# The last stage of a two-layer graph network: y0 in a second one-hot, edge weights two pairs ahead, both tiles in one VectorE instruction

## The reference, cut to what matters

```python
x0, x1 = _lin_irreps(x0, x1, W_up0, W_up1)        # 128 scalars and 128 x 3 vectors per node
tpw = h @ W_mlp4 / jnp.sqrt(...)                  # h: (E, 64), a radial network of edge_attr_8
w1, w2, w3, w4 = jnp.split(tpw, 4, axis=-1)       # 128 each
s0, s1 = x0[sender], x1[sender]
y0, y1 = edge_attrs[:, 0:1], edge_attrs[:, 1:4]
p1 = w1 * s0 * y0
p2 = (w2 * s0)[:, :, None] * y1[:, None, :]
p3 = w3[:, :, None] * s1 * y0[:, None, :]
p4 = w4 * jnp.einsum('eum,em->eu', s1, y1) / SQRT3
msg0 = segment_sum(concat([p1, p4]), receiver)
msg1 = segment_sum(concat([p2, p3]), receiver)
o0, o1 = _lin_irreps(msg0, msg1, W_out0, W_out1)
```

## Time and profile before

| what | value |
|---|---|
| median of 3 runs | 5701.41 us (5696.20 to 5704.77) |
| the profiled execution | 5664.33 us, span of the core 5662.4 us |
| granted TensorE clock, mean of the span | 0.938 |
| PE busy | 4809.4 us (85%) |
| VectorE (DVE) busy | 2867.7 us (51%) |
| ScalarE (ACT) busy | 2291.3 us (40%) |
| GpSimd (POOL) busy | 2726.7 us (48%) |
| chain that ended last | PE 30%, issue 24%, DVE 11%, DVEq 8%, ACT 7%, ACTq 7% |

### The profile page before, as it was taken

How to read it: one execution, slowest core, us unless ns; L and a number is a source line. 1 busy time by engine, 2 the same in 40 slices (tenths; PEclk the granted TensorE clock), 3 DMA queues, 4 the chain that set the end, 5 groups by cost and what they waited for, 6 DMA issues and landing times.

```text
span 5662.4 us, 106923 instructions
## 1 busy us (share of the span) xinstructions
PE 4809.4 (85%) x17040; PEld 2243.0 (40%) x17041; DVE 2867.7 (51%) x8231; ACT 2291.3 (40%) x6164; POOL 2726.7 (48%) x3492
## 2 busy tenths in 40 slices
PE   7898566778898878887788899999999999998998
PEld 5443122333343223333344444444444444444444
DVE  7543122334453111123344577777777777777676
ACT  0442000111112223431223466666666666666565
POOL 0333666776664655456666344433333333333332
PEclk9998677899998889998899999999999999999999
DMA  2233666777776767667777444444433343333333
GB/s 83 95 106 112 178 191 205 222 227 234 238 246 191 214 207 220 195 208 236 249 254 267 148 119 115 116 116 118 120 112 115 117 120 113 115 117 113 113 117 95
DMA packets 433675, 916.83 MB, mean 162 GB/s; under 512 B 63093, under 2 KB 170869, under 8 KB 433510
## 3 DMA queue, kind: packets, MB, share of 16 engines
q0 software_dynamic: 195840, 641.89, 38.0%
q1 hardware_dynamic: 182918, 245.65, 13.0%
q10 hardware_dynamic: 54880, 28.91, 1.7%
HBM read 787.79 MB, written 128.41 MB: 162 GB/s over the span
## 4 chain that ended last, share of the span: by engine, by line
PE 30%; issue 24%; DVE 11%; DVEq 8%; ACT 7%; ACTq 7%; POOL 4%; DMA 3%; another core or an unknown queue 3%; POOLq 2%; SPq 0%
PE bank L1267 8%; POOL ring L544 4%; PE bank L1392 3%; PE bank L1223 3%; PE bank L1225 3%; ACT hB L788 3%; ACTq L785 3%; ACT dense_w L799 3%; DVEq L1110 2%; DVE hA L1118 2%; DVE hA L1104 2%; DVEq L1120 2%; DMA ef<-in_ef_t_dram 2%; PE bank L1310 2%
## 5 line engine op out<-in xcount | busy, mean ns | idle before, releaser
L544 POOL DMA_INDIRECT ring<-tab_d,idx x1568 | 1549.7, 988 | 817.4 <-issue 523.2
L1392 PE MATMUL bank<-dense_w,oh 128*128 128x512 f32 x3520 | 1618.6, 602 | 71.2 <-DVE dense_w L1127 70.3
L1267 PE MATMUL bank<-ring,ohp 128*128 x3904 | 1105.4, 436 | 462.0 <-POOLq L556 226.2
L510 POOL DMA_INDIRECT ring<-up_d,idx x880 | 856.7, 973 | 498.5 <-POOL idx L506 348.4
L799 ACT ACTIVATE dense_w<-hA,hC 128x128 f32<-128x128 f32 x2640 | 820.0, 389 | 664.4 <-DVE hA L1118 599.5
L1392 PEld LDWEIGHTS bank<-dense_w,oh 128*128 128x128 f32 x3520 | 632.8, 189 | 863.0 <-issue 666.7
L1267 PEld LDWEIGHTS bank<-ring,ohp 128*128 x3904 | 411.3, 107 | 1134.2 <-issue 866.0
L1015 DVE TENSOR_TENSOR ohp<-iota_w,dst_f 128x512 f32 x392 | 266.5, 692 | 679.8 <-PE bank L1267 246.3
L506 POOL COPY idx<-src_i 128x2 int32 x440 | 80.5, 183 | 1054.3 <-DVE dense_w L1127 1012.2
L1382 PE MATMUL bank<-w,hC 64*128 64x256 f32 x3520 | 504.6, 404 | 31.5 <-issue 20.9
L1104 DVE SCALAR_TENSOR_TENSOR hA<-ring,hC,hB 128x128 f32<-128x128 f32 x880 | 270.9, 349 | 500.9 <-ACT hB L788 436.6
(11 more groups left out here) (180 smaller groups left out, 4917.6 us busy)
## 6 DMA issues: line engine op xcount, KB each, us to landing
hC<-hid_d SPq DMA_DIRECT2D x440, 64.0 KB
tab_d<-tout SPq DMA_DIRECT2D x98, 256.0 KB, 2.8
tw<-tab_d SPq DMA_DIRECT2D x98, 256.0 KB
hlw<-hl_d SPq DMA_DIRECT2D x98, 256.0 KB
ring<-tab_d,idx POOLq DMA_INDIRECT x1568
hid_d<-hC ACTq DMA_DIRECT2D x98, 256.0 KB
hl_d<-agg SPq DMA_DIRECT2D x74, 256.0 KB, 3.1
ring<-up_d,idx POOLq DMA_INDIRECT x880
```

Of the source, the lines that this page charges most:

```text
L510: g_.indirect_dma_start(ring_v[:, b, k, :], None, table, bass.IndirectOffsetOnAxis(idx_t[:, b, k:k + 1], 0)).then_inc(S["got"][b], 16)
L544: g_.indirect_dma_start(ring_h[:, b, k, :], None, table, bass.IndirectOffsetOnAxis(idx_b[:, b, k:k + 1], 0)).then_inc(S["got"][b], 16)
L1267: ins = pe.matmul(bank[0][:, :], ohp_b[:, bass.ds(at, 1), k, :].rearrange("p b n -> p (b n)"), ring_b[:, bass.ds(slot, 1), k, h, :].rearra ...
L1392: ins = pe.matmul(bank[h][:, :], oh[:, b, k, :], msg[:, b, k, h, :], start=False, stop=False, skip_group_check=True)
```

## The change

PSUM becomes one tensor `ps` of eight banks, so that an instruction may take both tiles' banks at once. The edge weights of a pair go into two neighbouring banks, and there are two such sets (banks 2 and 3, 4 and 5); PE issues them 512 columns wide, behind the sum of the pair two back. ScalarE no longer makes `w13`; it makes `oh0` = one-hot * y0 (two, 128 wide), and PE sums the half with p1 and p3 with `oh0` and the half with p4 and p2 with `oh`. VectorE starts a pair with the one-hot, `t2` and p1, goes on with q1, a drain and q2, then p3 for each tile, a drain and p4; it takes both tiles in one instruction for `t2`, p1 and p4; p3 reads w3 from PSUM. The zero matmuls that closed a window's banks go, the last sum closes them itself. In the order of windows, the second pair of each window is written out ahead of `copy_mT(w-1)`, and PE has the first two steps written out ahead of `out_product`. The minimum number of pairs in a window is now 4 (`MINV`).

The diff, cut to its core; its parts are in the order PSUM, ScalarE (`weigh`, `window`), VectorE (`messages`), PE:

```diff
+MINV = 4
-        bank = [ctx.enter_context(nc.psum_tensor(f"bank{i}", [P, D], F32)) for i in range(8)]
+        ps = ctx.enter_context(nc.psum_tensor("bank", [P, 8, D], F32))
+        bank = [ps[:, i, :] for i in range(8)]
-        w_bank = [[bank[2], bank[3]], [bank[7], bank[5]]]
-        m_bank = [bank[4], bank[6]]
+        w_bank = [ps[:, 2:4, :], ps[:, 4:6, :]]
+        m_bank = [bank[6], bank[7]]
...
-                    ac.wait_ge(M["w_done"], n + 2)
-                    ac.wait_ge(M["u_used"], n + (NU - 1))
-                    for k in range(2):
-                        ins = ac.mul(w13[:, k, :], w_bank[k][0][:, 0:2 * P], yg[:, b, 4 * k:4 * k + 1])
-                    ins.then_inc(M["w13"], 1)
                     ac.wait_ge(M["t2"], n)
                     ac.wait_ge(M["seg_done"], n)
                     for k in range(2):
                         for m in range(3):
-                            ins = ac.mul(msg[:, b, k, 1, P + m * P:2 * P + m * P], t2[:, k, :],
-                                         yg[:, b, 4 * k + 1 + m:4 * k + 2 + m])
+                            ac.mul(msg[:, b, k, 1, P + m * P:2 * P + m * P], t2[:, b, k, :],
+                                   yg[:, b, 4 * k + 1 + m:4 * k + 2 + m])
+                    for k in range(2):
+                        ins = ac.mul(oh0[:, b, k, :], oh[:, b, k, :], yg[:, b, 4 * k:4 * k + 1])
                     ins.then_inc(M["p2"], 1)
...
+                second_pair(w)
+                if not isinstance(w, int) or w > 0:
+                    copy_mT(w - 1)
                 rest(w)
                 if not isinstance(w, int) or w < NW - 1:
                     first_pair(w + 1)
                 keep_a(w)
-                copy_mT(w)
...
+                    w = w_bank[b]
+                    ve.wait_ge(M["seg_done"], n)
+                    ve.tensor_tensor(oh[:, b, :, :], iota_w[:, :].unsqueeze(1).broadcast_to([P, 2, P]),
+                                     dst_f[:, bass.ds(g * 2, 2)].unsqueeze(2).broadcast_to([P, 2, P]), ALU.is_equal)
+                    ve.wait_ge(M["got"][ub], ve.snap((n + (NU - 1)) // NU * 32))
+                    ve.wait_ge(M["w_done"], n + 2)
+                    ve.tensor_tensor(t2[:, b, :, :], w[:, :, 2 * P:3 * P], u[:, :, 0:P], ALU.mult).then_inc(M["t2"], 1)
+                    ve.tensor_tensor(msg[:, b, :, 0, 0:P], w[:, :, 0:P], u[:, :, 0:P], ALU.mult)
                     ve.wait_ge(M["q0"], n)
...
-                    ve.wait_ge(M["p2"], n)
                     for k in range(2):
-                        ins = ve.tensor_tensor(t2[:, k, :], w_bank[k][1][:, 0:P], u[:, k, 0:P], ALU.mult)
-                    ins.then_inc(M["t2"], 1)
-                    ve.drain()
-                    for k in range(2):
-                        ins = ve.tensor_tensor(msg[:, b, k, 1, 0:P], q2[:, k, :], w_bank[k][1][:, P:2 * P], ALU.mult)
-                    ins.then_inc(M["w_read"], 1)
-                    ve.wait_ge(M["w13"], n + 1)
-                    for k in range(2):
-                        ve.tensor_tensor(msg[:, b, k, 0, 0:P], w13[:, k, 0:P], u[:, k, 0:P], ALU.mult)
+                        ve.tensor_tensor(msg[:, b, k, 0, P:].rearrange("p (m u) -> p m u", m=3),
+                                         w[:, k, P:2 * P].unsqueeze(1).broadcast_to([P, 3, P]),
+                                         u[:, k, P:4 * P].rearrange("p (m u) -> p m u", m=3), ALU.mult)
                     ve.drain()
+                    ve.tensor_tensor(msg[:, b, :, 1, 0:P], q2[:, :, :], w[:, :, 3 * P:4 * P], ALU.mult).then_inc(M["u_used"], 1)
...
-                pe.wait_ge(M["w_read"], n)
-                pe.wait_ge(M["w13"], n)
-                for h in range(2):
-                    for k in range(2):
-                        ins = pe.matmul(w_bank[k][h][:, 0:2 * P], hid[k * HID:(k + 1) * HID, b, :],
-                                        w4[k * HID:(k + 1) * HID, h * 2 * P:(h + 1) * 2 * P], start=True, stop=True)
+                if not isinstance(n, int):
+                    pe.wait_ge(M["u_used"], n + (NU - 2))
+                for k in range(2):
+                    ins = pe.matmul(w_bank[b][:, k, :], hid[k * HID:(k + 1) * HID, b, :],
+                                    w4[k * HID:(k + 1) * HID, :], start=True, stop=True)
...
+                        ins = pe.matmul(bank[h][:, :], (oh0, oh)[h][:, b, k, :], msg[:, b, k, h, :], start=False,
+                                        stop=(last and k == 1), skip_group_check=True)
...
+                def one(b):
+                    sum_pair(n, b, last)
+                    if ahead:
+                        edge_weights(n + 2, b)
...
+                step(True)
+                if not isinstance(w, int) or w < NW - 1:
+                    step(True)
+                    if not isinstance(w, int) or w > 0:
+                        out_product(w - 1)
+                    with pe.Fori(lo + 2, hi - 1) as g:
+                        step(True)
+                    step(True, True)
-                touch(bank[0][:, :], D, False)
-                touch(bank[1][:, :], D, False).then_inc(M["sum_done"], 1)
```

More of the change, by code:

```diff
@@ L176, in build @@
         yg = hC[:, 1, 0:16].rearrange("p (b n) -> p b n", b=2)
-        w13 = hA[:, 0, :].rearrange("p (k n) -> p k n", k=2)
-        t2, q1 = (hA[:, 1, i * 256:(i + 1) * 256].rearrange("p (k n) -> p k n", k=2) for i in range(2))
+        t2 = hA[:, 0, :].rearrange("p (b k n) -> p b k n", b=2, k=2)
+        q1 = hA[:, 1, 0:256].rearrange("p (k n) -> p k n", k=2)
+        oh0 = yb[:, :].rearrange("p (b k n) -> p b k n", b=2, k=2)
         q2 = hB[:, 0, 0:256].rearrange("p (k n) -> p k n", k=2)
@@ L809, in first_pair, with second_pair @@
                 weigh(lo)
+            def second_pair(w):
+                weigh(ac.snap(lo_r) + 1)
             def rest(w):
-                with ac.Fori(ac.snap(lo_r) + 1, ac.snap(hi_r)) as g:
+                with ac.Fori(ac.snap(lo_r) + 2, ac.snap(hi_r)) as g:
                     weigh(g)
             def keep_a(w):
-                ac.wait_ge(M["sum_done"], w + 1)
+                more = 1 if isinstance(w, int) and w == NW - 1 else 0
+                ac.wait_ge(M["seg_done"], ac.snap(c) + more)
                 after(ac, M["turned"], w)
@@ L822, in copy_mT @@
                 after(ac, M["o_done"], w)
-                ac.copy(mT[:, 0:4, :], bank[4][:, :].rearrange("p (c n) -> p c n", c=4)).then_inc(M["mT_a"], 1)
+                ac.copy(mT[:, 0:4, :], m_bank[0][:, :].rearrange("p (c n) -> p c n", c=4)).then_inc(M["mT_a"], 1)
             def window(w):
+                second_pair(w)
+                if not isinstance(w, int) or w > 0:
+                    copy_mT(w - 1)
                 rest(w)
@@ L1138, in first_pair, with second_pair @@
                 messages(lo)
+            def second_pair(w):
+                messages(ve.snap(lo_r) + 1)
             def rest(w):
-                with ve.Fori(ve.snap(lo_r) + 1, ve.snap(hi_r)) as g:
+                with ve.Fori(ve.snap(lo_r) + 2, ve.snap(hi_r)) as g:
                     messages(g)
@@ L1147, in keep_b @@
             def keep_b(w):
-                ve.wait_ge(M["sum_done"], w + 1)
+                more = 1 if isinstance(w, int) and w == NW - 1 else 0
+                ve.wait_ge(M["seg_done"], ve.snap(c) + more)
                 after(ve, M["turned"], w)
@@ L1178, in _ @@
             over_windows(ve, window)
+            copy_mT(NW - 1)
             finish(NW - 1)
@@ L1391, in sum_pair @@
                     for h in range(2):
-                        ins = pe.matmul(bank[h][:, :], oh[:, b, k, :], msg[:, b, k, h, :], start=False, stop=False,
-                                        skip_group_check=True)
+                        ins = pe.matmul(bank[h][:, :], (oh0, oh)[h][:, b, k, :], msg[:, b, k, h, :], start=False,
+                                        stop=(last and k == 1), skip_group_check=True)
                 ins.then_inc(M["seg_done"], 1)
@@ L1417, in out_product, with step @@
                 ins.then_inc(M["o_done"], 1)
-            def weights_ahead():
+            def step(ahead, last=False):
                 n = pe.snap(c)
-                def step(b):
-                    edge_weights(n, b)
-                    sum_pair(n - 1, 1 - b)
-                pick(pe, pe.snap(n % 2), 0, 2, step)
+                def one(b):
+                    sum_pair(n, b, last)
+                    if ahead:
+                        edge_weights(n + 2, b)
+                pick(pe, pe.snap(n % 2), 0, 2, one)
                 pe.reg_add(c, c, 1)
```

42 lines of the change are left out of this document (16 added, 26 removed).

## The result

| | median, us | runs | against the kernel before (95%) |
|---|---|---|---|
| before, beside it | 5703.1 | 5696.2 to 5709.4 | |
| after | 5534.7 | 5512.9 to 5543.1 | 0.9699 [0.9669, 0.9729] |

The profiled execution after took 5543.1 us (span 5541.2).

The account below looks back on a forecast made before the run. A chain between VectorE and ScalarE was taken as the bound, with PE nearly full. Plain pairs -22 us, window changes -82, 5 given back: 5602 us against the median 5701.4; 8-in-10 range 5500 to 5715.

Parts of the forecast that it names:

- The ring: Last stage: VectorE waits for ScalarE's q0 (411 us), ScalarE's products for VectorE's t2 (584 us); the change cuts this.
- PE's own repeat of 4.60: PE in a plain pair: edge weights to sum 1.07 us plus the sum 3.53 us, so PE alone could repeat in 4.60.
- The restart of 1.5: VectorE, from issuing p4 to the next pair's first instruction: taken as 1.5 us, bounds 1.14 and 1.9, mostly open time.
- my own range: Forecast's range for the whole time, with the restart between 1.3 and 1.65 us and window bounds: 5540 to 5670 us.
- VectorE becomes the bound and the plain repeat hardly moves: Plain pairs of the last stage: VectorE's 4.90 us over PE's 4.60, against 4.95 before, giving -22 us.
- The first rival: Plain pairs: PE is the bound because the restart hides; repeat 4.60 us, 5477 us in all, chance 0.13.
- Edge weights to sum 1.07, side by side: PE, four 512-column edge-weight instructions with the two 64-row halves running together: 1.07 us, bounds 0.95 to 1.8.
- Changes of window 4.1 us: Last stage: each change costs 4.1 us extra instead of 5.8, 48 x -1.7 = -82 us, bounds -43 and -120.
- The 5 us given back: Added to the summed -104 us for the one-hot's wait and addresses: 5 us.
- Code fetch, 0.10: Rival: VectorE's window code is fetched again, 1.3 to 2.8 us per window, +61 to +132 us, 5663 to 5734; chance 0.10.
- The dearer restart: Rival: VectorE takes 1.9 us from p4 to the next pair, repeat 5.27 us, 5760 us; chance 0.09.
- the halves lose their overlap: Rival: PE's 64-row edge-weight halves no longer run side by side at 512 columns, repeat 5.25 us, 5793 us; chance 0.03.

Follow-up runs that it names:

- t2 first, alone: The kernel before with only t2 moved to the head of the pair, in two buffers: 5572.5 us, ratio 0.9807.
- the run with one wide product less: The changed kernel with the wide product p3 made for the first tile alone, so part of the messages is left out: 5483.6 us, ratio 0.9612.
- tile by tile: The changed kernel with t2, the first product and p4 made in two 128-column instructions each instead of one of 256: 5621.5 us, ratio 0.9875.
- second one-hot: The changed kernel with VectorE writing one more one-hot of the same kind to scratch in each pair: 5920.2 us, ratio 1.0378.

## Why the prediction was right or wrong

- *The ring is cut.* Right: t2 first, alone, gave the plain repeat its whole gain.
- *PE's own repeat of 4.60.* Short by 0.09. I read the sum's 3.53 up to a zero matmul; up to the 64-row edge weights it is 3.63. The earlier trace rows already showed 3.60 (4008.39 to 4011.99), and the prediction does not use it.
- *The restart of 1.5.* This term failed. It is 1.34 in the mean, from 1.07 to 1.51 by copy. I added ScalarE's longest path to VectorE's, though some of the four copies have shorter ones. With 3.32 to p4, VectorE repeats in 4.66. The lower end of my own range, 5540, does not follow from the 1.3 that it names either: 3.37 + 1.3 + 0.03 = 4.70 gives 440 x -0.25 - 82 + 5 + 5701 = 5514, so the result would have lain inside.
- *"VectorE becomes the bound and the plain repeat hardly moves."* Wrong, and it follows from the two terms before: 4.90 against 4.60 was really 4.66 against 4.69. Instead of 22 us the plain repeat gave about 114. The first rival, PE as the bound, is what happened, at 4.69 and not 4.60: with its repeat its own sum would have been 440 x -0.26 - 70 + 5701 = 5517. Its condition, that the restart hides, was needed only by 0.03 us.
- *Edge weights to sum 1.07, side by side.* Right: 1.06.
- *Changes of window 4.1 us.* 4.5, so 62 us (54 by the count) and not 82. The picture was right that VectorE's chain and its copy of bank 1 stand on the path: the run with one wide product less showed it.
- *The 5 us given back.* Nothing shows them apart.
- *Code fetch, 0.10.* It didn't happen here, but it is real: two of the kernels near this one had it. I priced it at 1.3 to 2.8 us a window; it cost 5.2 (0.0434 x 5700 / 48) and 4.4 (by the other), since there are two stretches of 3 us, where I had priced one transfer, and PE's clock falls behind them.
- *The dearer restart* and *the halves lose their overlap* did not happen.

The two large errors were of opposite sign: plain pairs 92 us too dear, changes of window 20 us too cheap. Their difference and the 5 us given back make 77, against the 67 us between 5602 and 5535. So that the time came out near the range is partly luck: the engine that bounds the plain repeat was named wrongly, and the error at the changes of window took back a part of what that cost.

## What to carry to other kernels

When two engines come out within a few tenths of a microsecond of each other, the sum has no bound to name (here 4.90 against 4.60 was 4.66 against 4.69): measure a repeat up to the very instruction that follows in the new order, and price both engines' levels. Where a loop restarts behind a drain, try queued work after the drain: with it the restart cost nothing in two of these kernels. When a small addition costs much, count where: here most of it lay at the changes of window and not in the plain repeat. Where a loop's body is long, look at the instruction packets of every build: a slower result may be the place of the code and not the edit.

## What the hardware showed that I had not expected

- Two empty stretches of 3.25 and 2.98 us on VectorE in a pass of the loop over windows, with 257 instruction packets instead of 31, removed by 32 drains ahead of the loop.
- Each switch of PE between 128-row and 64-row weights cost 0.09 to 0.10 us.
- The restart behind a drain differs by the copy that is chosen, from 1.07 to 1.51 us in the rows above.
- PE's granted clock fell to 0.50 behind idle stretches of 2.10 us (tile by tile) and 3.50 us (second one-hot), and stayed at 1.00 behind the 1.71 us of the changed kernel.
- One copied column per pair cost 39 us in all: 0.06 us on VectorE itself (3305.96 to 3306.02 in its order of time) and 0.17 us in a longer restart, in the pairs where VectorE sets the pace.
